# Two attention stages of a transformer kernel: one pool of eight PSUM banks, value products further behind, row products one unit earlier

## The reference

```python
x = x + 0.5 * ffn0(layernorm(x))    # stage 0, "f0": 512 -> 1536 -> 512, gate, up, down; fp8-rounded weights
x = x + attn0(layernorm(x))         # stage 1, "a0": 16 query heads, 4 key/value heads of 32, rope-like factor, biases
x = x + 0.5 * ffn0(layernorm(x))    # stage 2
x = x + 0.5 * ffn1(layernorm(x))    # stage 3, "f1": 512 -> 2048 -> 512
x = x + attn1(layernorm(x))         # stage 4, "a1": 16 heads of 32
x = x + 0.5 * ffn1(layernorm(x))    # stage 5

def attention(q, k, v):             # per batch and head, 1024 x 32 each
    att = einsum('qd,kd->qk', q, k) / sqrt(32)
    att = softmax(where(causal, att, -inf))
    return einsum('qk,kd->qd', att, v)    # then heads side by side times the output weights
```

## Time and profile before

| | |
|---|---|
| median of 3 runs | 2860.18 us (2854.9 to 2863.33) |
| profiled execution, its own time | 2862.99 us |
| its span, first to last instruction | 2861.3 us |
| mean granted TensorE clock | 0.982 |
| TensorE busy | 2681.4 us, 94% of the span |
| VectorE, ScalarE, GpSimd busy | 1371.1, 1082.3, 636.8 us |
| attention stage 1, first key product to last row product | 355.5 to 866.8 us |
| attention stage 4, the same | 1742.3 to 2296.8 us |

### The profile page before, as it was taken

How to read it: one execution, slowest core, us unless ns; L and a number is a source line. 1 busy time by engine, 2 the same in 40 slices (tenths; PEclk the granted TensorE clock), 3 DMA queues, 4 the chain that set the end, 5 groups by cost and what they waited for, 6 DMA issues and landing times. The chain is left out here.

```text
span 2861.3 us, 35927 instructions
## 1 busy us (share of the span) xinstructions
PE 2681.4 (94%) x13216; PEld 2014.1 (70%) x13216; DVE 1371.1 (48%) x2784; ACT 1082.3 (38%) x1989; POOL 636.8 (22%) x1102
## 2 busy tenths in 40 slices
PE   6999899888988999999999999988998899999999
PEld 5788655555546888888888886555655568888887
DVE  7777555645565444533333344555355643333333
ACT  7554355544554223411212134445444541211211
POOL 3333331222122224411111131121111231111110
PEclk9999899999999999999999999999999999999999
DMA  4221211121111110000000003221122200000001
GB/s 144 66 78 52 67 31 31 34 53 31 31 42 60 33 41 8 27 26 22 29 23 23 23 25 81 63 52 40 33 59 59 54 27 26 23 30 23 23 23 59
DMA packets 59678, 119.80 MB, mean 42 GB/s; under 512 B 11632, under 2 KB 12656, under 8 KB 59504
## 3 DMA queue, kind: packets, MB, share of 16 engines
q1 hardware_dynamic: 59504, 117.51, 14.8%
HBM read 62.42 MB, written 13.63 MB: 27 GB/s over the span
## 5 line engine op out<-in xcount | busy, mean ns | idle before, releaser
L735 PE MATMUL psum<-hA_hi,wmem 128*128 128x256 f32 (+1 forms) x1536 | 406.7, 336 | 9.3 <-DVE s1a0negmax L1197 3.3
L735 PEld LDWEIGHTS psum<-hA_hi,wmem 128*128 128x128 f32 x1536 | 270.3, 191 | 44.9 <-DVE s1a0negmax L1197 6.6
L735 PE MATMUL psum<-hA_lo,wmem 128*128 128x512 f32 (+1 forms) x864 | 294.2, 341 | 0.0
L1197 DVE CUSTOM_DVE_ANT_0 s4a1masked<-psum,mask_q 128x640 bf16<-128x640 f32 (+7 forms) x256 | 190.4, 753 | 155.4 <-PE psum L820 106.5
L1026 ACT ACTIVATE s1a0e<-psum,p_scale 128x384 f32<-128x384 f32 (+5 forms) x384 | 205.8, 584 | 156.1 <-PE psum L838 154.9
L1026 ACT ACTIVATE s4a1e<-psum,p_scale 128x384 f32<-128x384 f32 (+5 forms) x384 | 205.8, 584 | 148.0 <-PE psum L838 146.7
L1197 DVE CUSTOM_DVE_ANT_0 s1a0masked<-psum,mask_q 128x640 bf16<-128x640 f32 (+7 forms) x256 | 190.1, 754 | 111.9 <-PE psum L820 75.5
L1149 DVE SCALAR_TENSOR_TENSOR x<-psum,x 128x512 f32<-128x512 f32 x256 | 175.6, 688 | 86.2 <-PE psum L735 81.9
L1120 DVE TENSOR_TENSOR s5f1prod<-psum,s5f1silu 128x512 f32<-128x512 f32 x64 | 44.2, 691 | 299.0 <-PE psum L735 299.0
L1120 DVE TENSOR_TENSOR s3f1prod<-psum,s3f1silu 128x512 f32<-128x512 f32 x64 | 44.2, 691 | 294.5 <-PE psum L735 294.5
L735 PE MATMUL psum<-s3f1w,s3f1a 128*128 128x512 f32 x768 | 181.0, 391 | 0.9 <-POOL s3f1w L1296 0.9
(11 more groups left out here) (196 smaller groups left out, 5084.2 us busy)
## 6 DMA issues: line engine op xcount, KB each, us to landing
s1a0qst<-s1a0qs SPq DMA_DIRECT2D x96, 128.0 KB, 2.3
s4a1qst<-s4a1qs SPq DMA_DIRECT2D x96, 128.0 KB, 2.4
s4a1kst<-s4a1ks SPq DMA_DIRECT2D x96, 128.0 KB, 2.4
raw<-in_gate SPq DMA_DIRECT2D x44, 256.0 KB, 2.8
raw<-in_up SPq DMA_DIRECT2D x44, 256.0 KB, 2.8
raw<-in_down SPq DMA_DIRECT2D x44, 256.0 KB, 2.8
rounded<-s0f0w SPq DMA_DIRECT2D x24, 256.0 KB, 2.0
s2f0w<-rounded SPq DMA_DIRECT2D x24, 256.0 KB, 5.1
```

Source lines behind the costliest of these rows:

```text
L735: ins = pe.matmul(out_, w, m, start=n == 0, stop=n == len(terms) - 1)
L1197: dve.tensor_tensor_reduce(T[s]["masked"][turn % 2][:, 0:width].rearrange("p (z w) -> p z w", **bare), scores, mask_q[:, SEQ - width:SEQ]. ...
```

## The change

- `AHEAD` goes from 12 to 13: 13 row units run in front of the first key unit. The first row product of a head is then that of tile 3 (`FIRST_ROW`), the last that of tile 2. The job of the turned maxima gets one more empty place, so `m_tp` and `m_lo` stay at the same units.
- `PV_LAG` goes from 3 to 7, so the value products are taken off the list four units later than before: tiles 0 and 1 of a head come in unit 7 of that head (before in unit 3), tiles 6 and 7 in unit 5 of the next head (before in unit 1). `take`, `y_turn`, `y_fin`, `y_tp` follow four units later, `oproj` five.
- The weights of `oproj` are fetched two units earlier, the values of the second batch four units later.
- `bank_turns()` gives all eight banks from one pool, and takes the bank (or pair) that was *emptied* longest ago, by the place in the plan of the step that empties it.

```diff
-AHEAD = 12
+AHEAD = 13
 FIRST_ROW, LAST_ROW = -AHEAD % ST, (ST - 1 - AHEAD) % ST
-PV_LAG = 3
+PV_LAG = 7
...
                 if i == ST - 1:
-                    side.start([[], [("m_tp", s, n)], [("m_lo", s, n)]])
+                    side.start([[], [], [("m_tp", s, n)], [("m_lo", s, n)]])
...
-            put([split(s, "o", g, 0)], at + 25, 0)
+            put([split(s, "o", g, 0)], at + 23, 0)
...
         if grouped:
-            put(values(1), HEADS * ST - 3, 3)
+            put(values(1), HEADS * ST + (PV_LAG + 1) // 2 * 2 - 7, 3)
         else:
-            put(values(1), HEADS * ST - 4, 1)
+            put(values(1), HEADS * ST + (PV_LAG + 1) // 2 * 2 - 8, 1)
...
-                    job += [[("y_tp", s, g, 0)], [("y_tp", s, g, 1)]]
+                    job += [[("y_tp", s, g, 0)], [("y_tp", s, g, 1)], []]
                     job += [[("oproj", s, g, t)] for t in range(ST)]
...
+BANKS = 8
+EMPTIED_BY = {"piece": "piece_out", "v_tile": "v_out", "v_turn": "v_out", "m_tp": "m_lo",
+              "y_turn": "y_fin", "ln_tp": "ln_lo"}
...
+def banks_wanted(step):
+
+    kind = step[0]
+    if kind == "gu":
+        return 2
+    if kind == "row":
+        return 1 + ((step[-1] + 1) * P > CH)
+    if kind == "pv":
+        return int(step[-1] == 0)
+    return int(kind in ("key", "down", "ln_tp", "piece", "v_tile", "v_chunk", "v_turn", "m_tp",
+                        "y_turn", "y_tp", "oproj"))
...
 def bank_turns(plan):
 
-    banks, earlier, used = {}, {}, {}
-    slots, accs, acc_at = list(range(6)), [6, 7], 0
...
-            age = {bank: n for n, bank in enumerate(slots)}
-            first = min(range(6 - width + 1),
-                        key=lambda i: max(age[j] for j in range(i, i + width)))
...
-        elif kind == "down" or kind == "pv" and step[3] == 0:
-            mine = [accs[acc_at % 2]]
-            acc_at += 1
+    at = {step: now for now, step in enumerate(plan)}
+    banks, earlier, used, empty = {}, {}, {}, [-1] * BANKS
+    for now, step in enumerate(plan):
+        width = banks_wanted(step)
+        if not width:
+            continue
+        first = min(range(BANKS - width + 1), key=lambda i: max(empty[i:i + width]))
+        mine = list(range(first, first + width))
...
+        if step[0] == "pv":
+            then = at[("take",) + step[1:-1]]
         else:
-            continue
...
+            then = at[(EMPTIED_BY.get(step[0], step[0]),) + step[1:]]
         for bank in mine:
-            used[bank] = step
+            used[bank], empty[bank] = step, then
```

More of the change, by code:

```diff
@@ L355, in nth @@
         return self.place[step]
-def bank_turns(plan):
-    banks, earlier, used = {}, {}, {}
-    slots, accs, acc_at = list(range(6)), [6, 7], 0
-    for step in plan:
-        kind = step[0]
-        width = 0
-        if kind in ("gu",) or kind == "row" and (step[3] + 1) * P > CH:
-            width = 2
-        elif kind in ("ln_tp", "piece", "v_tile", "v_chunk", "v_turn", "row", "m_tp", "key",
-                      "y_turn", "y_tp", "oproj") or kind == "down" and step[4] >= 2:
-            width = 1
-        if width:
-            age = {bank: n for n, bank in enumerate(slots)}
-            first = min(range(6 - width + 1),
-                        key=lambda i: max(age[j] for j in range(i, i + width)))
-            mine = list(range(first, first + width))
-            for bank in mine:
-                slots.remove(bank)
-                slots.append(bank)
-        elif kind == "down" or kind == "pv" and step[3] == 0:
-            mine = [accs[acc_at % 2]]
-            acc_at += 1
-        else:
-            continue
-        banks[step] = mine
-        earlier[step] = [(used[bank], k) for bank, k in
-                         ((b, used.get(b) and banks[used[b]].index(b)) for b in mine)
-                         if bank in used]
@@ new lines, in bank_turns @@
+def bank_turns(plan):
+    at = {step: now for now, step in enumerate(plan)}
[6 more added lines that the diff above has]
+        mine = list(range(first, first + width))
+        banks[step] = mine
+        earlier[step] = [(used[bank], banks[used[bank]].index(bank)) for bank in mine
+                         if bank in used]
+        if step[0] == "pv":
+            then = at[("take",) + step[1:-1]]
+        else:
+            then = at[(EMPTIED_BY.get(step[0], step[0]),) + step[1:]]
```

## The result

| | before | after |
|---|---|---|
| median of 4 runs each | 2860.98 us | 2704.99 us (2697.1 to 2707.04) |
| ratio, 95% interval | | 0.9453 (0.9428 to 0.9477) |
| profiled execution, its own time | 2862.99 us | 2707.04 us |
| mean granted TensorE clock | 0.982 | 0.993 |
| first key to last row product, stage 1 | 511.3 us | 434.7 us |

The account below looks back on a forecast made before the run. It took TensorE as the bound, with 118.2 us idle in two attention loops, mostly waiting for banks emptied late. Terms 48 + 28 - 15 + 13 - 4 = 70 us off the median of 2860.18 gave 2790 us, range 2752 to 2845.

Parts of the forecast that it names:

- its signs: For both loops: listed waits under 10 us, idle 45 to 60 us, clock 0.98 or more, `negmax` largest; feed-forward unchanged.
- Banks: In both attention loops, giving banks by emptying place wins 85% of 56.0 us behind `y`, `mrow`, `hA_lo`: 48 us.
- the second kind: Other 62 us idle in both loops (other row maxima, exponentials, smaller rows, data waits): 45% won, 28 us.
- Order of the value products: Value products moved to other units of the attention loops: same cost, under 1 us less waiting, counted as 0.
- Rows one unit earlier: At group and stage starts, waits for stacked rows 3 us, one more row maximum 1 us: 4 us lost; bounds 0 and 37.
- What is given back: TensorE reaches the next bank earlier, leaving engines less time: 15 us lost; bounds 0 and half of 76 us.
- Clock: Of 37.5 us of full clock lacking in the two attention loops, a third returns: 13 us; bounds 0 and 30.
- The slower rival: Stacked rows come too late at 14 group boundaries, 37 us, plus lost clock: 2872 us; chance 0.05.
- more comes back: Nearly all bank waits in the loops go and the clock hardly falls: 104 us off, 2755 us; chance 0.10.

Follow-up runs that it names:

- pool_job: The changed kernel with PV_LAG 3 instead of 7, so value products stay at units 3, 5, 7 and 1; ratio 0.9603, 114 us off.
- order_only: The changed kernel with the old rule for banks (six by age of giving, two in turn); ratio 0.9791, 60 us off the kernel before.
- eight_given: The changed kernel with all eight banks taken by when last given out, only the value products' bank by its emptying; ratio 0.9567, 124 us off.
- six_two_emptied: The changed kernel with banks split six and two as before, but taken by the emptying step; ratio 0.9589, 118 us off.

## Why the prediction was wrong

Its mechanism held: banks given out before they are emptied were the largest part, and its signs came but for one. The waits behind `y`, `mrow` and `hA_lo` are 0 (foretold: under 10 us), the granted clock of the loops is 0.99 and 1.00 (0.98 or more), row products behind `negmax` are the largest group, and the feed-forward stages are unchanged. The idle time fell further than foretold, to 29.7 us and not 45 to 60. The sum was 86 us short. Step by step:

- **Banks** (48 + 28 - 15, and 13 for the clock: 74 us). The banks alone gave 90. The waits behind `y`, `mrow` and `hA_lo` went whole, 67 us with the smaller rows, where 48 stood in the sum. The 28 us of the second kind did not come: the other idle time grew by 15 us, for instance projections behind row maxima from 3.3 to 11.6 and row products behind exponentials in stage 4 from 9.1 us to 13.7. The clock gave 13.5 (40.1 to 26.6). What the sum had no term for is short stalls, 20 us (82 to 62): as I read them, waits for a bank that are shorter than the modelled end of the product before, which idle time doesn't show.
- **Order of the value products** (0 us). This is the step that failed, together with a term that was never in the sum, the earlier fetch of the output weights: 66 us lie between the banks alone and the whole change. I asked what the value products themselves wait for (under 1 us, and that was right) and whether VectorE and ScalarE still fit. I did not ask what TensorE waits for in the units that they leave and enter. With the banks alone TensorE stands behind exponentials with row products (2.1 + 13.7 us), behind row maxima with `oproj` and the other projections (10.4 + 1.2), behind `qs` with projections (3.0) and behind row maxima with `m_tp` (1.8 + 1.0): 33 us. In the changed kernel the same groups have 1.2 us. That is 32 of the 36.5 us by which the idle time differs; the clock (26.6 to 5.1) gives 21 more, short stalls 6. The groups end by different parts of the order. The 15.8 us behind exponentials go with the earlier fetch, since the weights' transfer held ScalarE; those of `oproj` with the empty place or with the lag; those of `m_tp` with `AHEAD`. The later value products by themselves, with all else in place, give 42 us (`pool_job` to the changed kernel, 114 to 156), 23 of them idle time: waits for the stacked keys fall from 10.3 to 2.0 us, row products behind row maxima from 25.4 to 16.6, projections behind `qs` from 4.8 to 0. What the fetch is worth by itself in time, no run shows; it and the empty place have 28 us at a lag of 3.
- **Rows one unit earlier** (-4 us). Right in what it rests on: the waits for the stack are 2.0 us, and at a lag of 3 they are 10.3, so the later value products cover them, as said. Not seen was that the earlier rows let `m_tp` off the last row maximum: 19.0 us of waits, 16 us of time, and only beside the late value products, since they bring that wait.
- **What is given back** (15 us). With the banks alone it came, and at this size: the 15 us above. The sum has it next to 28 us that did not come. In the whole change it is not to be seen: the idle time fell by 88.5 us, more than the 76 without it.
- **Clock** (13 us). 33 to 35 us came back, over the upper bound of 30. I took a third since long gaps at group boundaries would stay; but 41 of 47 waits over 1 us are gone.

The slower rival's mechanism, keys stacked too late, is real where the lag stays at 3, but at 10.3 us in 5 waits and not 37. The rival "more comes back" was nearest, and still 50 us short, for it too had the order at nothing. (Its 104 us give 2756 us from the median, not 2755, and the 11 us of "slower" give 2871, not 2872; nothing hangs on it.)

Not settled is why the clock and the short stalls fall with each part as they do: on the whole they fall as the waits do, but no run changed one of them by itself, and `order_only` has less lost clock than the kernel before with as many long waits. Nor was a lag over 7 tried, or the earlier fetch alone.

## What to carry to other kernels

Give a buffer by when it is emptied, and let all users share one pool: on this order either gave some 60 us and both 96. When a kernel's engines each run one strict order, moving a long piece of work must be costed by what it stood between and what it stands between afterwards, not by its own waits; here that was 42 us for a move costed at nothing. A wait of TensorE behind ScalarE can have a transfer behind it, so follow a wait one engine further, as with the output weights here. Where the bounding engine is pipelined, count on more than its idle time: 88 us less of it in two loops came with 158 us off their length, with the clock and the stalls that count as busy.

## What the runs showed of the hardware

**The sum of idle time alone does not tell how much clock is lost.** `eight_given` and `six_two_emptied` have the same idle time in the loops, from their windows of stage 1 and 4:

```profile
351.90:807.40 455.50, 424.11 (x2512) 270.72 (x2512) 289.39 (x751) 259.30 (x519) 124.86 (x320) 0.97 0.17 40
1689.80:2181.00 491.20, 466.31 (x2866) 315.80 (x2864) 284.59 (x743) 279.67 (x557) 114.52 (x312) 0.99 0.24 58
```

```profile
352.60:811.00 458.40, 421.73 (x2512) 266.34 (x2513) 290.78 (x751) 260.43 (x519) 124.47 (x320) 0.99 0.17 40
1689.60:2177.50 487.90, 467.79 (x2867) 312.14 (x2866) 284.31 (x743) 279.74 (x557) 114.17 (x312) 1.00 0.25 59
```

31.4 + 24.9 = 56.3 us in the first, 36.7 + 20.1 = 56.8 in the second. But within the loops the first has 39.2 us of it in 33 waits of over 1 us, and the second 8.3 us in 6 and the rest in short ones; the granted clock is 0.97 and 0.99 in the one, 0.99 and 1.00 in the other, 16.5 us lost against 3.4. This is one trace of each. The one of `eight_given` is the slowest of its four executions, whose mean clock is 0.990 to 0.997, while those of `six_two_emptied` have 0.996 and 0.997, so part of the difference is chance and its size is not shown. In the kernel before, each of the 16 falls to 1.2 GHz that begin in the loops came within 3 us of the end of one wait of 1.1 to 2.3 us. Most long waits had no fall: there are 44 of over 1 us in these loops. And in the changed kernel one fall, at 1710.6, had only waits of 0.49, 0.14 and 0.11 us shortly before. Four of the 16 falls (1794.9, 1863.2, 2102.1 and 2173.8) came with the waits behind exponentials for which ScalarE had first stood 2.0 to 2.5 us for the transfer of the output weights.

The Trainium skill, "TensorE: Matmul & The Clock Gate", has both sides of it. Its section "A second HAM failure mode: psum-queue depth-cycling" tells of a matrix engine that stops briefly between groups as it goes round the banks of PSUM, and so loses its clock again and again; the trace of before agrees, with 16 falls, and the trace of after has two. The prediction held against the neighbouring section "HAM oscillation — how this bites in real kernels", where double-buffered PSUM gave no further gain once the loop had been reordered, that its case waits for transfers and this one hardly does. That holds for TensorE's own waits. But four of the falls have a transfer behind ScalarE, so both kinds are here; and two more banks in the pool gave 64 us.
